# Scores of a 64 wide attention as two passes of 128 rows instead of three of 64

## The chip, the core and the metric

The kernel runs on one core of one Trainium2 chip. It is written by hand for the five engines of a core: TensorE (PE, matmuls), VectorE (DVE), ScalarE (ACT), GpSimd (POOL) and SyncE (SP, which here only begins transfers). Each engine works through its own queue of instructions in order, and the queues meet at semaphores. The metric is the time of one execution on the device, in microseconds (us); lower is better.

## The reference

It is a decoder of four layers on x of 8 x 256 x 256 in float32; each layer adds a gated cross attention to a context of 8 x 256 x 192 and a gated feed forward part of its own kind. The change lies in the third layer's cross attention, with 16 heads of 64:

```python
def _L2_xattn_ref(x, context, w_q, w_k, w_v, w_o, b_o):
    HEADS = 16
    DIM_HEAD = 64
    ...
    SCALE = DIM_HEAD ** (-0.5)
    q = (x @ w_q).reshape(B, Sq, HEADS, DIM_HEAD).transpose(0, 2, 1, 3)
    k = (context @ w_k).reshape(B, Skv, HEADS, DIM_HEAD).transpose(0, 2, 1, 3)
    v = (context @ w_v).reshape(B, Skv, HEADS, DIM_HEAD).transpose(0, 2, 1, 3)
    sim = jnp.einsum('bhid,bhjd->bhij', q, k) * SCALE
    attn = jax.nn.softmax(sim, axis=-1)
    out = jnp.einsum('bhij,bhjd->bhid', attn, v)
    out = out.transpose(0, 2, 1, 3).reshape(B, Sq, INNER)
    return out @ w_o + b_o
...
    x = x + jnp.tanh(g_xattn[2]) * _L2_xattn_ref(_layernorm(x, axis=-1), ctx_768, ...)
```

## The kernel before

The stages run one after the other: l0x, l0f, l1x, l1f, l2x, l2f, l3x, sim, l3f (an x is an attention, an f a feed forward part). The change edits l2x, which the class `Wide` plans and the functions `wide` of each engine carry out, and one load of weights for l3f.

Matmuls whose result must be close to float32 are done with operands split into two parts, a high part (rounded to the format fp32r) and a low part (the rest). `mm3` adds three passes: low by high, high by low, high by high. The product of the two low parts is left out.

l2x goes through 128 heads: 8 batch items of 16. Four neighbouring heads (index `u`) share one set of tiles: `keys2[u % 3]` and `queries2[u % 3]`, 128 partitions high, where an even head of each couple has partitions 0 to 63 and an odd one 64 to 127 (`e = i % 2`), and `k = i // 2 % 2` says which couple. For step i, TensorE's queue has in this order:

- `scores(i)`: for both halves of the queries (t) one `mm3` of 64 rows, 128 x 256 each, into bank i % 2; six matmuls
- `turn_probs(i - 3)`: four transposes (line 2005) of the normalised probabilities of head i - 3
- the jobs of step i: keys of u = i // 4 + 2 at i % 4 = 0, values (v) at 1, queries at 2, nothing at 3; in each item moreover at i % 16 = 5 and 6 the two halves of the output projection of the item before (`projected`, line 1979), and at 7 the transposes of the next item's rows
- at odd i, the product of probabilities and values for two heads (line 2020), which writes 64 columns at a time

VectorE in step i: the row maxima of head i (line 1037), the copy of the transposed probabilities of head i - 3 (line 1044), then what the jobs of step i - 1 ask for: `low_keys` (line 1052) or `low_queries` (line 1060); at i % 16 = 1 also `combine` (line 943, adding the mixture of the layer before) and the statistics for the next item; at 7 `finish`, whose first operation (line 1075, the sum with the bias) sets the bank of the output projection free. ScalarE: the high parts of keys and queries (`high_keys`, `high_queries`), copies of values and outputs, and the exponentials of head i (line 1620). GpSimd: division by the sum (lines 837 and 840), the splitting of the context, and at i % 16 = 3 four gathers of rows (line 769). SyncE begins the loads of the context, one for each item.

The products of jobs go to the banks 5, 6 and 7 in turn (`place`), and TensorE waits (`mf`) until the product that had the bank before has been read. The keys and queries of u are jobs eight and six steps ahead of the first scores that read them; `scores(i)` waits until the exponentials of head i - 2 have read its bank.

## Time and profile before

| | before |
|---|---|
| median of 3 runs | 2401.87 us (2387.91 to 2403.25) |
| the profiled execution | 2405.62 us |
| its span in the profile | 2403.9 us |
| mean granted TensorE clock | 0.868 of full speed |
| busy in the span: PE / PEld / DVE / ACT / POOL | 1970.7 / 1529.6 / 1316.6 / 769.3 / 782.9 us |
| HBM read and written | 89.26 and 47.19 MB |
| the l2x stage in the span | from about 1045 to 1513 us |

PE is the matmuls, PEld the loading of their stationary operand, which overlaps them. The profile is of one execution; its rows give starts and durations of instructions from the start of the span. The shares of busy time are over all stages together, and say little of one of them.

### The profile page before, as it was taken

How to read it: one execution, taken by the hardware profiler on the slowest of the kernel's cores; microseconds unless marked ns; L12 is line 12 of the kernel's file. 1: busy time of each engine (PE TensorE's matmuls, PEld its weight loads, DVE VectorE, ACT ScalarE, POOL GpSimd, SP SyncE). 2: the span in 40 equal slices, each digit the busy share in tenths (PEclk: the TensorE clock that was granted, in tenths of full speed). 3: DMA queues.
4: the chain of work that ended last, by engine and by line, in shares of the span. 5: the costliest groups of instructions: out<-in, count | busy, mean ns of one | idle time of the engine just before them, and what ended most of it. 6: DMA issues, size and time to landing. Idle time of an engine off the chain costs nothing.

```text
span 2403.9 us, 33562 instructions
## 1 busy us (share of the span) xinstructions
PE 1970.7 (82%) x12232; PEld 1529.6 (64%) x12232; DVE 1316.6 (55%) x2824; ACT 769.3 (32%) x1697; POOL 782.9 (33%) x694
## 2 busy tenths in 40 slices
PE   3589699942999999869999999599967888448997
PEld 2467566532777777757778787478855555336664
DVE  2434478551555444345555555565546898446773
ACT  1122146400222121134444444122322445112554
POOL 4110101054355444256666555454533200100000
PEclk9789679655999999879999999599985889776898
DMA  4280456123333332220000001034626542023341
GB/s 142 84 279 0 58 77 88 22 81 116 110 110 119 110 110 92 82 68 16 13 13 13 4 1 66 3 105 136 205 78 112 86 66 29 0 36 56 57 74 41
DMA packets 120190, 177.88 MB, mean 74 GB/s; under 512 B 10916, under 2 KB 105188, under 8 KB 117412
## 3 DMA queue, kind: packets, MB, share of 16 engines
q1 hardware_dynamic: 91092, 128.36, 23.4%
q0 software_dynamic: 8448, 26.52, 3.7%
q10 hardware_dynamic: 20496, 20.97, 2.6%
q8 instruction: 95, 1.56, 0.3%
q14 instruction: 59, 0.48, 0.1%
HBM read 89.26 MB, written 47.19 MB: 57 GB/s over the span
## 4 chain that ended last, share of the span: by engine, by line
PE 59%; issue 12%; DVE 11%; POOL 9%; DMA 5%; ACT 2%; SPq 1%; DVEq 0%; POOLq 0%; ACTq 0%
PE bank L1846 13%; PE bank L1847 10%; PE bank L1848 10%; PE bank L2125 5%; PE bank L2157 4%; POOL ewl L785 3%; DMA ew<-in_we 3%; PE bank L2005 3%; PE bank L2020 3%; PE bank L1979 2%; DVE nmf L1144 2%; PE bank L2142 1%; POOL ewh L783 1%; POOL rows_by_expert L797 1%; PE bank L2167 1%
## 5 line engine op out<-in xcount | busy, mean ns | idle before, releaser
L1144 DVE TENSOR_REDUCE nmf<-bank 128x2 f32<-128x512 f32 x384 | 260.8, 689 | 120.4 <-PE bank L2125 117.6
L1719 ACT ACTIVATE pT<-bank 128x512 f32<-128x512 f32 x384 | 224.8, 597 | 249.6 <-PE bank L2142 247.6
L1407 DVE TENSOR_TENSOR bank<-sil,bank 128x512 f32<-128x512 f32 x136 | 94.8, 697 | 285.0 <-ACT sil L1774 284.5
L2125 PE MATMUL bank<-kpack,qpack 48*128 48x256 f32 (+1 forms) x768 | 202.1, 370 | 53.6 <-DVE nmf L1144 30.9
L1846 PE MATMUL bank<-split,ewl 128*128 128x512 f32 x514 | 212.1, 413 | 24.2 <-POOL ewl L785 13.9
L1847 PE MATMUL bank<-split,ewh 128*128 128x512 f32 (+1 forms) x578 | 228.7, 396 | 0.0
L1848 PE MATMUL bank<-split,ewh 128*128 128x512 f32 (+1 forms) x578 | 227.7, 394 | 0.0
L2125 PEld LDWEIGHTS bank<-kpack,qpack 48*128 48x128 f32 (+1 forms) x768 | 128.6, 222 | 134.8 <-DVE nmf L1144 63.9
L785 POOL TENSOR_TENSOR ewl<-ew,ewh 128x1536 fp32r<-128x1536 f32 (+1 forms) x47 | 205.9, 4380 | 3.8
L2142 PE MATMUL bank<-qpack,kpack 50*128 50x256 f32 (+1 forms) x768 | 198.5, 359 | 9.2 <-ACT pT L1719 9.1
L783 POOL CAST ewh<-ew 128x1536 fp32r<-128x1536 f32 (+1 forms) x47 | 85.2, 1813 | 325.0 <-DMA ew<-in_we 314.3
L1037 DVE TENSOR_REDUCE nmax<-bank 128x2 f32<-128x512 f32 x128 | 88.5, 691 | 186.8 <-PE bank L1848 186.3
L1620 ACT ACTIVATE w<-bank,nmax 128x256 f32<-128x256 f32 x256 | 119.2, 471 | 223.1 <-DVE nmax L1037 223.0
L1774 ACT ACTIVATE sil<-bank 128x512 f32<-128x512 f32 x136 | 81.4, 598 | 322.0 <-PE bank L1848 322.0
L1846 PE MATMUL bank<-ewh,split 128*128 128x256 f32 x544 | 168.1, 309 | 6.6 <-issue 6.6
L1847 PE MATMUL bank<-ewl,split 128*128 128x256 f32 x544 | 156.6, 288 | 0.0
L1848 PE MATMUL bank<-ewh,split 128*128 128x256 f32 x544 | 156.1, 287 | 0.0
L724 POOL TENSOR_TENSOR rstd<-rstd,mhalf 128x2 f32<-128x2 f32 x40 | 28.5, 712 | 385.2 <-DVE rstd L1128 256.4
L837 POOL TENSOR_TENSOR esum<-esum,minus 128x2 f32<-128x2 f32 x128 | 89.3, 698 | 168.1 <-ACT w L1620 167.9
L840 POOL TENSOR_TENSOR w<-w,esum 128x512 f32<-128x512 f32 x128 | 137.0, 1070 | 10.1
L2142 PEld LDWEIGHTS bank<-qpack,kpack 50*128 50x128 f32 (+1 forms) x768 | 124.0, 212 | 24.5 <-ACT pT L1719 19.9
L1846 PEld LDWEIGHTS bank<-split,ewl 128*128 128x128 f32 x514 | 98.1, 191 | 63.2 <-DVE split L1410 21.1
(431 smaller groups left out, 4757.7 us busy)
## 6 DMA issues: line engine op xcount, KB each, us to landing
ew<-in_we SPq DMA_DIRECT2D x32, 768.0 KB, 7.8
ew<-in_we SPq DMA_DIRECT2D x15, 1408.0 KB, 6.2
rows_by_expert<-zeros ACTq DMA_DIRECT2D x1, 20480.0 KB, 62.5
kpack<-khl SPq DMA_DIRECT2D x144, 128.0 KB, 4.0
qpack<-qhl SPq DMA_DIRECT2D x144, 128.0 KB
arena<-rows_by_expert SPq DMA_DIRECT2D x23, 512.0 KB, 4.2
rows_by_expert<-arena SPq DMA_DIRECT2D x38, 256.0 KB, 5.5
ct<-in_ctxT SPq DMA_DIRECT2D x32, 192.0 KB, 2.4
```

The lines of the kernel that those rows point to most:

```text
L783: nc.gpsimd.tensor_copy(high, whole).then_inc(m["wh"], 1)
L785: nc.gpsimd.tensor_tensor(low, whole, high, ALU.subtract).then_inc(m["ws"], 1)
L840: nc.gpsimd.tensor_tensor(p3, p3, total.rearrange("p (t o) -> p t o", o=1).broadcast_to([P, T, S]), ALU.mult).then_inc(m["pn"], 1)
L1144: V.tensor_reduce(nmf[:, c, :, j, r], bank[s.banks[i % len(s.banks)]][:, :] .rearrange("p (t k) -> p t k", t=T), AXX, ALU.max, negate=True ...
L1620: ins = A(probs[i % 4][:, t * S:(t + 1) * S], bank[i % 2][:, t * S:(t + 1) * S], ACT.Exp, bias=nmax[:, h, t:t + 1], accum_out=esum[:, h, t ...
L1719: A(pT16[i % 8][:, :], bank[2 + h % 2][:, :], ACT.Exp, scale=s.qscale).then_inc(m["e"], 1)
L1846: mm(out_, al, bh, start=start, stop=False)
L1847: mm(out_, ah, bl, start=False, stop=False)
L1848: return mm(out_, ah, bh, start=False, stop=stop)
L2125: ins = mm(bank[s.banks[i % len(s.banks)]][:, t * S:(t + 1) * S], q[rows, r, t * P:(t + 1) * P], k[rows, r, :], start=True, stop=True)
L2142: ins = mm(bank[2 + h % 2][:, t * S:(t + 1) * S], k[rows, r, t * P:(t + 1) * P], q[rows, r, :], start=True, stop=True)
L2157: ins = mm(bank[4][j * 32:j * 32 + s.vs, gr % 2 * S:(gr % 2 + 1) * S], v16[n % 3][:, kt, h * s.vs:(h + 1) * s.vs], pT16[(n * NH + (h ^ 1)) ...
```

## The change

The high and the low part of the queries now stand above each other: for the even head of a couple the high part in partitions 0 to 63 and the low part in 64 to 127, for the odd head the other way round (`queries2[u % 3][e]`). The keys' high part stands in both halves, and their low part in the half of the queries' high part, with zeros in the other. Then two passes of 128 rows do what three of 64 did: (high and low queries) by (high keys twice), and (high and low queries) by (low keys and zeros).

The parts are written where they are made, in two instructions of 64 partitions each instead of one of 128, by ScalarE (high) and VectorE (low; the low queries to the other half than they are read from). The second copy of the keys' high part is made by transfers from SBUF to SBUF, two for each u, which SyncE begins when ScalarE has written the high keys (`kh`), and for which the first scores of u wait (`kd0` to `kd2`). The zeros are written once at the start of the stage by six copies on VectorE (`kz`). SyncE's loads of the context move into the same loop. The tiles take more room: `rows3`, which now lies over `raw3`, holds some of the queries, and so the three loads of the l3f weights into `raw3` move from the kernel's start (line 718) to GpSimd's part of the l2f stage.

```diff
@@ -264,7 +265,8 @@
         raw1 = w13[:, 0:6 * D].rearrange("p (w c f) -> p w c f", w=3, c=DC)
-        raw3 = sb("raw3", [P, 3, DC, D])
+        raw3 = under("raw3", [P, 3, DC, D])
+        rows3 = sb("rows3", [P, 3 * DC * D], F32R)
         onx = [w13[0:NX, b * D:(b + 1) * D] for b in range(4)]
@@ -390,8 +392,10 @@
         wv2 = split[0:CK, 8192:8192 + 4 * inner].rearrange("p (w c f) -> p w c f", w=2, c=2)
-        keys2 = [t.rearrange("p (w g s) -> p w g s", w=2, g=2) for t in threes(0, 4 * S)]
-        queries2 = [t.rearrange("p (w g s) -> p w g s", w=2, g=2) for t in threes(3072, 4 * S)]
+        keys2 = [t.rearrange("p (e w g s) -> p e w g s", e=2, w=2, g=2) for t in threes(0, 8 * S)]
+        queries2 = [[t[:, o + e * 512:o + e * 512 + 512].rearrange("p (g s) -> p g s", g=2) for e in range(2)]
+                    for t, o in ((split, 6144), (rows3, 0))]
+        queries2.append([t[:, o:o + 512].rearrange("p (g s) -> p g s", g=2) for t, o in ((split, 7168), (rows3, 1024))])
         values2 = [arena[:, 12288 + k * 1024:13312 + k * 1024].rearrange("p (t n) -> p t n", t=T) for k in range(3)]
@@ -436,14 +440,14 @@
 
-        names = ("x_in", "w0_in", "w0f_in", "att_in", "consts", "tanh", "phase", "out_done", "w3_in", "w2a_in", "w2b_in", "w2c_in",
+        names = ("x_in", "w0_in", "w0f_in", "att_in", "consts", "tanh", "phase", "out_done", "w3_in", "w2a_in", "w2b_in", "w2c_in", "w4_in",
                  "xn", "xnT", "xt", "rq", "rd", "zero", "masked")
...
 
-        wx = group("l2x", "ct", "cs", "wh", "wl", "xh", "kh", "qh", "s", "mx", "e", "psum", "pn", "pT", "pTc", "pv", "oc", "dve",
+        wx = group("l2x", "ct", "cs", "wh", "wl", "xh", "kh", "kd0", "kd1", "kd2", "kz", "qh", "s", "mx", "e", "psum", "pn", "pT", "pTc", "pv", "oc", "dve",
                    "mp0", "mp1", "mp2", "mf0", "mf1", "mf2")
@@ -631,10 +635,16 @@
             if "l2x" in run:
-                for n in range(B):
-                    if n > 0:
-                        sp.wait_ge(wx["cs"], 2 * n)
-                    sp.dma_start(ct[:, :, :], a["ctxT"][n, :, :, :]).then_inc(wx["ct"], 16)
+                sp.dma_start(ct[:, :, :], a["ctxT"][0, :, :, :]).then_inc(wx["ct"], 16)
+                for u in range(L2X.pairs):
+                    sp.wait_ge(wx["kh"], u + 1)
+                    for e in range(2):
+                        own, other = slice(64 * e, 64 * e + 64), slice(64 - 64 * e, 128 - 64 * e)
+                        sp.dma_start(keys2[u % 3][other, e, 0, :, :].bitcast(F32),
+                                       keys2[u % 3][own, e, 0, :, :].bitcast(F32)).then_inc(wx[f"kd{u % 3}"], 16)
+                    if u % 4 == 0 and u // 4 + 1 < B:
+                        sp.wait_ge(wx["cs"], 2 * (u // 4 + 1))
+                        sp.dma_start(ct[:, :, :], a["ctxT"][u // 4 + 1, :, :, :]).then_inc(wx["ct"], 16)
             if "l2f" in run:
@@ -708,7 +718,7 @@
             later2 = [(raw2[0], a["wq_l2x"]), (raw2[1], a["wk_l2x"]), (raw2[2], a["wv_l2x"]), (wo["l2x"], a["wo_l2x"])]
-            loads += [(raw3[:, 0, :, :], a["wq_l3f"]), (raw3[:, 1, :, :], a["wk_l3f"]), (raw3[:, 2, :, :], a["wv_l3f"])]
+            later3 = [(raw3[:, 0, :, :], a["wq_l3f"]), (raw3[:, 1, :, :], a["wk_l3f"]), (raw3[:, 2, :, :], a["wv_l3f"])]
             loads += [(bo[n][:, :], a[f"bo_{n}"].partition_broadcast(P)) for n in ("l2x", "l3x", "l3f")]
@@ -802,6 +812,8 @@
                         pool.dma_start(dst, src).then_inc(g["w3_in"], 16)
+                    for dst, src in later3:
+                        pool.dma_start(dst, src).then_inc(g["w4_in"], 16)
                 for w in range(s.ring, s.sets):
@@ -874,6 +886,7 @@
                     root(sm, 2, ss[:, 0:NH], ss[:, 0:NH], mhalf[:, 0:NH])
+                    pool.wait_ge(g["w4_in"], 16 * 3)
                     split_packed(L3F)
@@ -1049,7 +1062,10 @@
                     src = from_[:, :].rearrange("p (g s) -> p g s", g=2)
-                    tt(keys2[u % 3][:, 1, :, :], src, keys2[u % 3][:, 0, :, :], ALU.subtract).then_inc(done, 1)
+                    for e in range(2):
+                        own = slice(64 * e, 64 * e + 64)
+                        ins = tt(keys2[u % 3][own, e, 1, :, :], src[own, :, :], keys2[u % 3][own, e, 0, :, :], ALU.subtract)
+                    ins.then_inc(done, 1)
 
@@ -1057,8 +1073,10 @@
                     src = from_[:, :].rearrange("p (g s) -> p g s", g=2)
-                    stt(queries2[u % 3][:, 1, :, :], src, s.qscale, queries2[u % 3][:, 0, :, :], ALU.mult, ALU.subtract)\
-                        .then_inc(done, 1)
+                    for e in range(2):
+                        own, other, to = slice(64 * e, 64 * e + 64), slice(64 - 64 * e, 128 - 64 * e), queries2[u % 3][e]
+                        ins = stt(to[other, :, :], src[own, :, :], s.qscale, to[own, :, :], ALU.mult, ALU.subtract)
+                    ins.then_inc(done, 1)
 
@@ -1081,6 +1099,11 @@
                 normal(0)
+                for u in range(3):
+                    for e in range(2):
+                        other = slice(64 - 64 * e, 128 - 64 * e)
+                        V.tensor_copy(keys2[u][other, e, 1, :, :], zeros[other, :, :].broadcast_to([64, 2, S]))\
+                            .then_inc(m["kz"], 1)
                 for i in range(s.FIRST, s.last):
@@ -1591,13 +1614,19 @@
                         act.wait_ge(m["s"], 4 * (u - 2))
-                    copy(keys2[u % 3][:, 0, :, :], groups(from_)).then_inc(m["kh"], 1)
+                    for e in range(2):
+                        own = slice(64 * e, 64 * e + 64)
+                        ins = copy(keys2[u % 3][own, e, 0, :, :], groups(from_)[own, :, :])
+                    ins.then_inc(m["kh"], 1)
 
...
                         act.wait_ge(m["s"], 4 * (u - 2))
-                    A(queries2[u % 3][:, 0, :, :], groups(from_), ACT.Copy, scale=s.qscale).then_inc(m["qh"], 1)
+                    for e in range(2):
+                        own = slice(64 * e, 64 * e + 64)
+                        ins = A(queries2[u % 3][e][own, :, :], groups(from_)[own, :, :], ACT.Copy, scale=s.qscale)
+                    ins.then_inc(m["qh"], 1)
 
@@ -1983,16 +2012,18 @@
                     u, k, e = i // 4, i // 2 % 2, i % 2
+                    if i == 0:
+                        pe.wait_ge(m["kz"], 6)
                     if i % 4 == 0:
...
                         filled(("q", u))
+                        pe.wait_ge(m[f"kd{u % 3}"], 32 * (u // 3 + 1))
                     if i >= 2:
                         pe.wait_ge(m["e"], i - 1)
-                    r = slice(64 * e, 64 * e + 64)
-                    for t in range(T):
-                        ins = mm3(bank[i % 2][:, t * S:(t + 1) * S],
-                                  [queries2[u % 3][r, w, k, t * P:(t + 1) * P] for w in range(2)],
-                                  [keys2[u % 3][r, w, k, :] for w in range(2)], True, True)
+                    for t in range(T):
+                        for w in range(2):
+                            ins = mm(bank[i % 2][:, t * S:(t + 1) * S], queries2[u % 3][e][:, k, t * P:(t + 1) * P],
+                                     keys2[u % 3][:, e, w, k, :], start=w == 0, stop=w == 1)
                     ins.then_inc(m["s"], 1)
```

TensorE's queue at the first scores of the second set (head 3, then head 4 of the first item; `split` and `rows` hold keys and queries, `ewh,ewl` are the query projections ahead, `ident,w` the transposes of probabilities). Before:

```order
L1848 MATMUL bank<-ewh,ewl 128x256
L1846 MATMUL bank<-split 128x256 [waits l2x_e]
L1847 MATMUL bank<-split 128x256
L1848 MATMUL bank<-split 128x256
...
L2005 MATMUL bank<-ident,w 128x128 [waits l2x_pn]
L2005 MATMUL bank<-ident,w 128x128 x3
L1846 MATMUL bank<-split 128x256 [waits l2x_e,l2x_mf0,l2x_mf1]
```

And in the changed kernel:

```order
L1877 MATMUL bank<-ewh,ewl 128x256
L2025 MATMUL bank<-split 128x256 [waits l2x_e]
L2025 MATMUL bank<-split 128x256 x3
L2036 MATMUL bank<-ident,w 128x128 [waits l2x_pn]
L2036 MATMUL bank<-ident,w 128x128 x3
L2025 MATMUL bank<-split,rows 128x256 [waits l2x_kd1,l2x_e,l2x_mf0,l2x_mf1]
```

Four matmuls stand in the place of six, and the first of a set has the transfers (`kd1`) among its waits.

VectorE's queue at the start of the stage, from behind the first normalised rows (`xn`) on (`ewh` are the low parts of the turned rows, `split` and `rows` the low keys and queries, `x<-w` the sums of `combine`). Before:

```order
L1032 TENSOR_SCALAR xn<-x,mv,rstd 128x256
L1068 TENSOR_TENSOR ewh<-bank,ewh 128x512 [waits l2x_xh,l2x_mp0]
L1052 TENSOR_TENSOR split<-bank,split 128x512 [waits l2x_kh,l2x_mp1]
L1060 SCALAR_TENSOR_TENSOR split<-bank,split 128x512 [waits l2x_qh,l2x_mp0]
...
L1037 TENSOR_REDUCE nmax<-bank 128x2 [waits l2x_s] x2
L1052 TENSOR_TENSOR split<-bank,split 128x512 [waits l2x_kh,l2x_mp1]
L943 SCALAR_TENSOR_TENSOR x<-w,gw_l1f,x 128x256 [waits mo_gt1]
```

And in the changed kernel:

```order
L1045 TENSOR_SCALAR xn<-x,mv,rstd 128x256
L1105 CAST split<-zeros 64x512 x6
L1086 TENSOR_TENSOR ewh<-bank,ewh 128x512 [waits l2x_xh,l2x_mp0]
L1067 TENSOR_TENSOR split<-bank,split 64x512 [waits l2x_kh,l2x_mp1]
L1067 TENSOR_TENSOR split<-bank,split 64x512
L1078 SCALAR_TENSOR_TENSOR split<-bank,split 64x512 [waits l2x_qh,l2x_mp0]
L1078 SCALAR_TENSOR_TENSOR split<-bank,split 64x512
...
L1050 TENSOR_REDUCE nmax<-bank 128x2 [waits l2x_s] x2
L1067 TENSOR_TENSOR split<-bank,split 64x512 [waits l2x_kh,l2x_mp1]
L1067 TENSOR_TENSOR split<-bank,split 64x512
```

Six copies of zeros have come in ahead of the low rows, and each low key or query operation has become two of half the height, of which the second pair shown now stands ahead of `combine`.

## Rows read from the trace of the kernel before

**Rows 1.** Stretch: us, busy PE, PEld, DVE, ACT, POOL, clock, DMA share, GB/s.

```profile
1172.00:1228.00 56.00, 56.00 (x380) 44.80 (x378) 31.97 (x58) 25.30 (x81) 34.29 (x40) 1.00 0.05 14
```

**Rows 2.** The chain that ended last: start us, us, what; l2x, output projection.

```profile
1185.85 3.46 PE bank L1979 x16
...
1242.11 3.46 PE bank L1979 x16
```

**Rows 3.** Timeline of PE, an odd head's scores: start, us, engine, line.

```profile
1209.08 0.28 PE L1848 MATMUL bank<-ewh,ewl 128*128 128x256 f32 x1
1209.29 0.38 PE L1846 MATMUL bank<-split 64*128 64x256 f32 x1
1209.52 0.28 PE L1847 MATMUL bank<-split 64*128 64x256 f32 x1
...
1209.99 0.27 PE L1848 MATMUL bank<-split 64*128 64x256 f32 x1
1210.19 0.66 PE L2005 MATMUL bank<-ident,w 128*128 128x128 f32 x4
```

**Rows 4.** Timeline of PE, start of l2x: queries end, keys of 96 rows begin.

```profile
1055.48 0.28 PE L1848 MATMUL bank<-ewh,ewl 128*128 128x256 f32 x1
1055.60 0.28 PE L1846 MATMUL bank<-ewh,ewl 96*128 96x256 f32 x1
1055.72 0.28 PE L1847 MATMUL bank<-ewh,ewl 96*128 96x256 f32 x1
```

**Rows 5.** Timeline of PE: four transposes that follow other transposes.

```profile
1198.02 0.60 PE L1970 MATMUL bank<-ident,xn 128*128 128x128 f32 x4
```

**Rows 6.** One VectorE line, two heights: ns min/median/max, first and last start.

```profile
L1407 DVE TENSOR_TENSOR bank<-sil,bank x136: 695/697/706, 594.3 to 1777.2; 128x512 f32<-128x512 f32 x121, 64x512 f32<-64x512 f32 x15
```

**Rows 7.** Timeline: head 1's scores begin, head 2's exponentials end, head 4's scores.

```profile
1170.69 0.38 PE L1846 MATMUL bank<-split 64*128 64x256 f32 x1
...
1178.73 0.20 ACT L1620 ACTIVATION_READ_ACCUMULATOR w<-bank,nmax 128x1 f32 x1
...
1179.99 0.38 PE L1846 MATMUL bank<-split 64*128 64x256 f32 x1
```

**Rows 8.** Timeline: head 7's maxima, bias sum of the output, key matmuls at head 8.

```profile
1197.63 0.69 DVE L1037 TENSOR_REDUCE nmax<-bank 128x2 f32<-128x512 f32 x1 [5.09 <-PE bank L1848]
...
1199.43 0.68 DVE L1075 TENSOR_TENSOR scr<-bank,bo_l2x 128x512 f32<-128x512 f32 x1
...
1200.88 0.36 PE L1846 MATMUL bank<-ewh,ewl 96*128 96x256 f32 x1
```

**Rows 9.** Transfers: KB each and median us to landing; six issues on SP's queue.

```profile
kpack<-khl SPq DMA_DIRECT2D x144, 128.0 KB, 4.0
...
276.52 3.92 SPq L594 DMA_DIRECT2D kpack<-khl  x6
```

**Rows 10.** Timeline of the stage's start: normalised rows, high keys, first queries, first scores.

```profile
1048.48 0.73 DVE L1032 TENSOR_SCALAR xn<-x,mv,rstd 128x256 f32<-128x256 f32 x2 [2.70 <-POOL rstd L724]
...
1052.97 0.60 ACT L1545 ACTIVATE split<-bank 128x512 fp32r<-128x512 f32 x1 [1.90 <-PE bank L1848]
...
1054.16 0.28 PE L1846 MATMUL bank<-ewh,ewl 128*128 128x256 f32 x1
...
1059.96 0.38 PE L1846 MATMUL bank<-split 64*128 64x256 f32 x1
```

**Rows 11.** Timeline of PE at head 6; the stretch around it.

```profile
1079.03 0.66 PE L2005 MATMUL bank<-ident,w 128*128 128x128 f32 x4 [1.57 <-POOL w L840]
...
1077.00:1091.00 14.00, 12.43 (x71) 10.06 (x71) 5.26 (x9) 5.24 (x16) 11.48 (x15) 0.76 0.09 25
```

**Rows 12.** Timeline of PE in the last eight heads: the longest wait there.

```profile
1484.61 0.65 PE L2020 MATMUL bank<-arena 128*64 128x256 f32 x4 [1.14 <-ACT w L1545]
```

**Rows 13.** The chain of waits at the kernel's start.

```profile
17.97 1.61 POOL raw L718 x3
...
26.44 2.95 POOL rstda L724
```

## The prediction

> **What bounds the kernel now.** I read the table of stretches first. In a stretch of 56 us in the middle of the l2x stage (the only stage whose loops the change edits) TensorE's matmuls are busy for all of it at the full granted clock, 2.4 GHz, while VectorE has work for 32 us, GpSimd for 34, ScalarE for 25 and the DMA engines for 5% [rows 1]. The chain of waits says the same: inside this stage it holds TensorE lines alone, and its row for the 16 output-projection matmuls comes back after 1242.11 - 1185.85 = 56.26 us [rows 2]. That is one batch item, 16 heads, so a head costs 3.52 us. What a head's matmuls cost is therefore what the stage costs, until another wait takes over.
>
> Next the timeline of one head [rows 3]. Inside a run of 256-column matmuls with 128 or 96 rows the starts lie 0.12 us apart, also where a run with other operands begins [rows 4]. The score batch has 64 rows and is different at both its ends. The first score matmul starts 1209.29 - 1209.08 = 0.21 us after the last query matmul, and the second 0.23 after the first: with 0.12 as the normal step this is 0.09 + 0.10 too much (other batches show 0.22 for the second). At the other end the transposes start 0.20 after the last score matmul, 0.08 too much, and four of them take 0.66 us, where four that follow transposes take 0.60 [rows 5]: 0.06 more. So a 64-row batch costs about 0.19 us on entry and 0.14 on exit, beside its six matmuls. An even head is entered from the value matmuls, which write only 64 columns, so that its entry is a change of shape either way. The Trainium skill (TensorEngine Tiling (Array Packing), Tiling Modes, Key Properties) says that changing the tiling mode drains the engine; the trace agrees, with the sizes above.
>
> **The change on TensorE.** (a) Two passes fewer for each half of the queries: 6 matmuls become 4, so a head saves 2 x 0.118 = 0.236 us. The new ones have 128 rows, whose step is 0.12 instead of 0.118; for 64 in a batch item I take off 0.1 us. (b) With 128 rows the exit from the scores to the transposes is no change of shape: 0.14 us a head. (c) The entry is none either at odd heads, where key or query matmuls come before: 0.19. At even heads the 64-column value matmuls still come before, and I leave the entry as it is. An even head saves 0.376 us, an odd one 0.566; 16 heads save 8 x 0.942 - 0.1 = 7.4 us. Without (b) and (c) it would be 3.7.
>
> **What it adds, and who waits.** Key and query parts are now written in two instructions of 64 partitions. An operation of VectorE on 64 partitions takes as long elsewhere as on 128, 695 to 706 ns over both forms [rows 6], and I take the same for ScalarE; so each of the two engines issues one more operation of 0.6 to 0.7 us for keys and one for queries, four times four heads: some 5 us of VectorE and 5 of ScalarE in 50, well inside their idle time. In order, though, two places come late:
>
> Head 2 of each item. After head 1's maximum VectorE does the low keys, then the sums of the previous layer and the statistics, and only then head 2's maximum. From head 1's first score matmul, 1170.69, to the end of head 2's exponentials, 1178.93, is 8.24 us; head 4's scores, which write the same bank, start at 1179.99, 9.30 after [rows 7]. The shorter batch takes 0.34 from the first number (0.10 + 0.236), the second key operation adds 0.6: 8.50, and 0.12 for the semaphore makes 8.62. TensorE would arrive at 9.30 - 0.476 - 0.376 - 0.566 = 7.88. New stall: 0.74 us.
>
> Head 8. The key matmuls after its transposes take the PSUM bank that VectorE frees with the bias sum of the output (L1075). From head 7's maximum, 1197.63, that sum ends at 1200.11, 2.48 after, and the key matmuls start at 1200.88, 3.25 after [rows 8]. With a second low-query operation ahead (0.6) and 0.1 for the semaphore the bank is free at 3.18; TensorE arrives at 3.25 - 0.14 - 0.376 = 2.73. New stall: 0.45 us.
>
> So an item costs 56.26 - 7.4 + 1.2 = 50.0 us, a gain of 6.2.
>
> The copies of the keys' high part: SyncE has nothing else queued then but the next context, whose wait is over by that time. Two issues at 3.92/6 = 0.65 us each and 4.0 us from issue to landing for 128 KB of the same kind (SBUF to SBUF) [rows 9] give some 5.5 us after ScalarE is done. The scores that read them come seven heads after, 7 x 3.05 = 21 us: hidden, at no cost. At head 0, where nothing has been built up, ScalarE begins the high keys at 1052.97 and is done with two operations by 1054.2, the second copy lands 0.65 + 4.0 later, near 1058.9, and the first scores begin at 1059.96 [rows 10]: 1 us to spare. The Trainium skill (DMA: Bandwidth & Descriptors, Anatomy of one DMA) has about 2 us of fixed cost for a DMA, which would only widen that margin; the row is of copies that queue behind each other, and is the one used.
>
> The six copies of zeros stand on VectorE between the first normalised rows and the first low rows. The trace has no such copy. Bounded by nothing and by 0.7 us each (a vector operation of this width, [rows 6]), they end 0 to 4.2 us after 1049.2, the low rows 0.7 later, by 1054.1 at the latest, and the queries that read those start at 1054.16 [rows 10]: between 0 and 0.1 us. I take 0.
>
> **Edges of the stage.** Heads 0 to 6 of the first item gain nothing: the transposes at 1079.03 wait 1.57 us for GpSimd [rows 11], which has four gathers ahead of that product, and that queue is paced by VectorE's sums. Heads 7 to 15: 0.476 + 4 x 0.376 + 4 x 0.566 = 4.2. Six items from head 16 to head 111: 6 x 6.2 = 37.3. Heads 112 to 119, which have no sums to wait for: 3.8. In the last eight heads there are no key or query matmuls left as cover, and every fourth head already waits for the output copy behind its exponentials [rows 12]; there a pair gains 0.33 instead of 0.94, so 2 x 0.33 + 2 x 0.94 = 2.5, and 2.4 with the odd start. Sum 47.7 us.
>
> **Outside the stage.** Three loads of l3f weights leave the start of GpSimd's queue, 1.61 us, and directly behind that queue stands the root that the first stage waits for, on the chain [rows 13]: 1.6 us gained. They come back in the l2f stage, behind the last scatter, where GpSimd next waits for weights that are loaded only once an expert is done: 0.
>
> Sum: 47.7 + 1.6 = 49.3. From the profiled execution's 2405.62 that gives 2356.3; its time is 3.75 above the median of the three, 2401.87, from which I forecast **2353 us**.
>
> **Rivals.** A, only the matmul count matters: the gaps at the ends of the batch belong to the semaphore waits there, not to the 64 rows. Then an item saves 3.7, with nearly no new stall (head 4: 9.30 - 3 x 0.236 = 8.6 against 8.6), so 6 x 3.6 + 9 x 0.236 + 8 x 0.236 + 1.5 + 1.6 = 28.7: 2373. Against it stand the key matmuls of [rows 4], which also begin behind waits and have no gap. 12%.
>
> B, the new stalls lower TensorE's clock. After the 1.57 us of idling the mean granted clock of 14 us was 0.76 [rows 11]: part of them passed at 1.2 GHz instead of 2.4, which lost 14 x 0.24 = 3.4 us of work. One such fall in each of six items gives back 20 us: 2373; two give 2393. Against it: a wait of 1.14 us in the last heads [rows 12] did not do it, and mine are 0.74 and 0.45. 8%. The Trainium skill (TensorE: Matmul & The Clock Gate, Part 1) tells of such falls after idle gaps; no gap of 0.7 us shows one here.
>
> C, slower: the copies land late. TensorE would wait at every fourth head for the landing. What is asked for seven heads ahead paces four heads at 4/7 of the landing time, and this exceeds today's 14.07 us for four heads from 24.6 us of landing on; at 26 us the stage would be some 25 us longer and the time 2427. The row says 4.0, and the engines are 5% busy. 2%.
>
> D, better: even heads lose their entry gap as well, 0.19 x 60 = 11 us: 2342. 7%.
>
> **How the numbers follow.** The forecast with its own errors (the new stalls between 0 and 2.5 us an item instead of 1.2, some 7 us either way, and about 2 for the edges) spans 2343 to 2363 and has 68%; another 3% are causes I can't name. The range of 8 in 10 leaves out C and the far end of B: 2341 to 2374. A measurement tells some 1% from no change, 24 us. Faster by more: the forecast, D and nearly all of A and B, 93%; within 1%: 5%; slower: 2%.
>
> **What would show it.** In the profile after: item period near 50.0 us in the chain; 512 score matmuls 0.12 apart, with no gap to the transposes; a gap of 0.1 left at even heads; waits of TensorE of 0.7 us for the exponentials at head 4 and 0.45 at head 8 in six items; no wait for the copies, with landings near 4 us; the root on GpSimd 1.6 us earlier. The forecast fails if the gaps stay (A), if the clock row falls below 1.00 in mid-stage (B), or if VectorE's half-height operations that move between halves take clearly more than 0.7 us.

## The result and the profile after

The changed kernel takes 2365.43 us, the median of four runs (2360.91 to 2370.63); the kernel before takes 2396.46 on the same chip (2387.91 to 2403.25). The ratio is 0.9873, with a 95% interval of 0.9842 to 0.9903: 31 us less. The forecast was 2353, a gain of 49 from a median of 2401.87 for the kernel before; a fourth run has since brought that median down by 5.4, so the time missed by 12 us and the gain by 18. The time is inside the range, but the gain is two thirds of what was forecast, and in the l2x stage, where it was to arise, it is smaller by a third too.

The profiled execution took 2362.5 us (span 2360.8, mean clock 0.869; before 2405.62, 2403.9 and 0.868). Stage by stage, from the marks of the two traces: the first root on GpSimd starts at 24.73 instead of 26.44; from the first statistics of l2x to the root of l2f it is 1473.69 - 1036.4 = 437.3 us instead of 1514.82 - 1045.5 = 469.3. That makes 1.7 + 32.0 = 33.7. The rest of the 43.1 us between the two spans comes from stages whose code is the same (3.4, 4.0, 0.8, -9.4 and 10.6 us): they scatter from one execution to the next, and nothing below rests on them.

First a head without disturbance, an odd one, on the timeline of PE. It answers to [rows 3]:

```profile
1142.63 0.28 PE L1877 MATMUL bank<-ewh,ewl 96*128 96x256 f32 x1
1142.75 0.64 PE L2025 MATMUL bank<-split,rows 128*128 128x256 f32 x4
1143.22 0.60 PE L2036 MATMUL bank<-ident,w 128*128 128x128 f32 x4
```

The score batch begins 0.12 us after the last key matmul, lasts 0.47 us (four steps of 0.12) and is followed by transposes that take 0.60. The gaps of 0.09 and 0.10 at its start and of 0.08 and 0.06 at its end are gone. An even head keeps the gap at its start, behind the value matmuls: there the batch shows 0.74 instead of 0.64.

The stage as a whole doesn't look like that. One batch item in a stretch of the table of windows, which answers to [rows 1], and below it the chain of waits, which answers to [rows 2] (its pieces of under 0.2 us are left out, as are longer ones at the marks):

```profile
1099.00:1150.70 51.70, 48.98 (x351) 40.87 (x349) 38.47 (x66) 29.60 (x90) 34.14 (x39) 1.00 0.14 35
```

```profile
1102.59 0.47 ACT split L1568
1103.07 0.30 ACT split L1568
1103.36 0.38 issue
1103.75 0.68 DVE split L1067
1104.44 0.69 DVE split L1067
1105.17 1.71 DVE x L956 x2
1106.91 0.88 DVE x L956 x2
...
1109.10 0.70 DVE nmax L1050
...
1110.44 1.08 PE bank L2051 x8
...
1116.36 3.46 PE bank L2008 x16
...
1168.03 3.46 PE bank L2008 x16
```

The period is 1168.03 - 1116.36 = 51.67 us (forecast 50.0, before 56.26), and TensorE is busy for 48.98 us of 51.7. Before, the chain held TensorE alone. Now at head 2 of every item it goes through ScalarE's two high-key copies, VectorE's two low-key operations, the sums of the previous layer (L956) and the statistics, and comes back to TensorE at a value product. (Its last link, of 0.2 us, lies on head 2's exponentials; but the value product waits in the code for `pTc`, VectorE's copy of turned probabilities, and the rows below name it.) The timeline of PE gives the size of that wait, and the view of PE's waits for 1036 to 1470 us (line that waited, on what; us in total, times, longest) how often it comes:

```profile
1110.44 1.08 PE L2051 MATMUL bank<-sil,arena 128*64 128x256 f32 x8 [2.11 <-DVE sil L1057]
```

```profile
PE bank L2051 <- DVE sil L1057: 13.4, 7, 2.1
PE bank L2025 <- ACT w L1649: 5.8, 2, 5.0
PE bank L2051 <- ACT w L1568: 4.3, 2, 3.2
PE bank L1875 <- DVE scr L1093: 3.7, 6, 0.6
```

Six of the seven in the first row are 2.11 us long, one in each item. The last row is the wait at head 8 that was forecast at 0.45. The second is mostly in the first item, where head 4 waits 5.0 us for the exponentials of head 2 (0.65 before), and the third in the last eight heads.

### The profile page after: what moved, and what is told of

Its sections match the earlier page's. It is cut to its first block, busy times and chain, and to the rows that moved or that the text cites. A ratio compares the mean times of both kernels' runs of the same rounds, so it can differ in the third digit from the quotient of the medians.

```text
span 2360.8 us, 33280 instructions
## 1 busy us (share of the span) xinstructions
PE 1904.9 (81%) x11976; PEld 1489.9 (63%) x11976; DVE 1368.9 (58%) x2894; ACT 803.2 (34%) x1761; POOL 779.7 (33%) x694
## 3 DMA queue, kind: packets, MB, share of 16 engines
q8 instruction: 93, 1.52, 0.3%
## 4 chain that ended last, share of the span: by engine, by line
PE 54%; issue 14%; DVE 13%; POOL 10%; DMA 5%; ACT 3%; SPq 1%; DVEq 0%; POOLq 0%; ACTq 0%
PE bank L1875 10%; PE bank L1876 8%; PE bank L1877 8%; PE bank L2156 6%; PE bank L2188 4%; POOL ewl L795 3%; DMA ew<-in_we 3%; PE bank L2008 2%; DVE nmf L1167 2%; PE bank L2025 2%; PE bank L2051 2%; PE bank L2173 1%; PE bank L2036 1%; POOL ewh L793 1%; POOL rows_by_expert L807 1%
```

## Experiments

Most readings below use the item period, from VectorE's bias sum of one item to that of the next (L1093, before L1075). It repeats within 0.04 us wherever the clock stays up, so it tells tenths of a microsecond where the medians tell 5 or 10. In the kernel before all six periods are 56.26; in the changed one they are 51.67, 53.21, 51.66, 51.68, 51.67 and 49.48. The last belongs to an item with no sums of a next one behind head 1: it is 2.19 us shorter, so the kernel itself holds the first hint.

**1. The sums one step later.**

```diff
-                    if i % 16 == 1 and 1 <= (i + 15) // 16 < B:
-                        combine(L1F, (i + 15) // 16, ch)
-                        statistics((i + 15) // 16)
+                    if i % 16 == 2 and 1 <= i // 16 + 1 < B:
+                        combine(L1F, i // 16 + 1, ch)
+                        statistics(i // 16 + 1)
```

> The changed kernel, with VectorE's combine and statistics of the next item one loop step later (behind the maximum and the turned copy of the loop step in which the value product of head 3's step finds its input). Baseline: the changed kernel at 2365.4 us, item period 51.67, step from head 3 to head 4 4.20 us. Theory 1 (the missing gain sits in VectorE's queue: half-height writers plus combine hold back the turned copy for which the value product waits 2.11 us): that wait goes, the step from 3 to 4 falls to 2.0 to 2.1; maximum 3 is late instead, and the scores of head 5 wait 0.5 to 1.3 us for its exponent. Item period 50.2 to 51.1, time 2353 to 2361. Rival 1 (it sits in ScalarE's halved writers, or PE pays for something that the trace hides): moving combine only moves the wait, item period stays at 51.5 to 51.9, time within 3 us of 2365. Rival 2 (the shorter stall is not on the path, other waits fill it): step 3 to 4 falls but the item period does not.

2359.44 us (2355.97 to 2360.58), ratio 0.9858 (0.9812 to 0.9903). The step from head 3 to head 4 fell from 4.20 to 2.02 us, and no value product waits for VectorE any more. But maximum 3 came late instead, then exponentials 3 to 5; the step from head 5 to head 6 grew from 6.86 to 7.90, with a new wait of the output projection for ScalarE's output copy, six times:

```profile
PE bank L2008 <- ACT w L1568: 4.5, 6, 0.7
PE bank L1875 <- DVE scr L1093: 3.7, 6, 0.6
PE bank L2051 <- ACT w L1568: 3.2, 1, 3.2
```

Item 50.54: of the 2.19 us, 1.13 were won back. The wait belongs to where the sums stand in VectorE's queue; the victim of the new place was another than I had named (the scores of head 5).

**2 and 3. Passes and rows apart.** Three passes of 128 rows, from the changed kernel (the low part of the keys counts twice in the scores):

```diff
-                        for w in range(2):
+                        for j, w in enumerate((0, 1, 1)):
                             ins = mm(bank[i % 2][:, t * S:(t + 1) * S], queries2[u % 3][e][:, k, t * P:(t + 1) * P],
-                                     keys2[u % 3][:, e, w, k, :], start=w == 0, stop=w == 1)
+                                     keys2[u % 3][:, e, w, k, :], start=j == 0, stop=j == 2)
```

> The changed kernel with a third matmul of 128 rows per tile (the low part of the keys counted twice in the scores), so three passes as before, but no 64-row matmul in the scores. Theory 1 (the gaps of 0.14 and 0.19 us belong to the 64-row layout): plain steps stand at 2.45+0.24=2.69, 2.02+0.24=2.26 and 3.40+0.24=3.64 where the kernel before has 2.93, 2.50 and 3.87; the stall of 2.11 us in each item shrinks to about 1.4 since PE is 0.7 us later by then. Item 51.67+3.8-0.7=54.8 against 56.26 before; time 2365+8*3.1=2390, 3 to 9 us under before. Rival 1 (the gaps belong to the waits at the heads' edges and not to the rows): plain steps as before, 2.93 and 2.50, the time at or above before. Rival 2 (stalls are independent of PE's pace): 2365+30=2396.

Two passes of 64 rows, from the kernel before (the product of low queries and high keys is left out):

```diff
-                        ins = mm3(bank[i % 2][:, t * S:(t + 1) * S],
-                                  [queries2[u % 3][r, w, k, t * P:(t + 1) * P] for w in range(2)],
-                                  [keys2[u % 3][r, w, k, :] for w in range(2)], True, True)
+                        for w in range(2):
+                            ins = mm(bank[i % 2][:, t * S:(t + 1) * S], queries2[u % 3][r, 0, k, t * P:(t + 1) * P],
+                                     keys2[u % 3][r, w, k, :], start=w == 0, stop=w == 1)
```

> The kernel before with the pass of low queries by high keys left out: two passes of 64 rows, nothing else changed (scores lack that product). Theory 1 (a pass is worth 0.236 us a head, the gaps stay): plain steps 2.93-0.24=2.69, 2.50-0.24=2.26, 3.87-0.24=3.63; the chain on VectorE is the old one (copy ready 0.5 us before its use, now 0.7 us earlier wanted), so a stall of 0.2 to 0.4 us a period. Item 56.26-3.8+0.3=52.8; time 2396-8*3.5=2368, 24 to 31 us under before. Rival 1 (gaps belong to waits): the same time, but then the run with three passes of 128 rows gains nothing. Rival 2 (the passes are the whole gain of the changed kernel): its steps are 2.45 and 2.02 and the item 51.7.

Timeline of PE at the same odd head, with three passes of 128 rows:

```profile
1148.37 0.28 PE L1877 MATMUL bank<-ewh,ewl 96*128 96x256 f32 x1
1148.49 0.88 PE L2025 MATMUL bank<-split,rows 128*128 128x256 f32 x6
1149.21 0.60 PE L2036 MATMUL bank<-ident,w 128*128 128x128 f32 x4
```

and with two of 64:

```profile
1141.87 0.28 PE L1848 MATMUL bank<-ewh,ewl 96*128 96x256 f32 x1
1142.08 0.73 PE L1994 MATMUL bank<-split 64*128 64x256 f32 x4
1142.74 0.66 PE L2005 MATMUL bank<-ident,w 128*128 128x128 f32 x4
1143.15 0.48 PE L1846 MATMUL bank<-split,ewh 96*128 96x512 f32 x1
```

Six matmuls of 128 rows have no gap at either end; four of 64 rows still have 0.21 us on entry and the longer exit. The waits at the heads' edges are the same in both, so the gaps belong to the rows. That settles rival A.

| | item, us | median, us | ratio (95%) |
|---|---|---|---|
| three passes of 64 rows (before) | 56.26 | 2396.9 | 1 |
| two passes of 64 rows | 52.50 | 2375.54 | 0.9931 (0.9904 to 0.9959) |
| three passes of 128 rows | 54.42 | 2387.64 | 0.9968 (0.9941 to 0.9995) |
| two passes of 128 rows (changed) | 51.67 | 2365.4 | 0.9873 (0.9842 to 0.9903) |

The pass alone gives 3.76 us an item, 16 x 0.236 = 3.78 as costed, and no wait of TensorE above 0.45 us appears with it in the items: the old VectorE queue is just fast enough for that pace. The rows alone give 1.84, with the value product waiting 1.2 us at head 3. Together they give 4.59 and not 5.6, because the faster TensorE runs into the longer queue. By the medians the pass alone gains 21 us (a little under the 24 to 31 expected) and the rows alone 9.

**4. No copies.** SyncE's two transfers for each four heads and the wait for them are out; the other half of the keys' high part holds zeros, written by six more copies at the stage's start, so one product is left out of the scores.

```diff
-                        sp.dma_start(keys2[u % 3][other, e, 0, :, :].bitcast(F32),
-                                       keys2[u % 3][own, e, 0, :, :].bitcast(F32)).then_inc(wx[f"kd{u % 3}"], 16)
...
-                        pe.wait_ge(m[f"kd{u % 3}"], 32 * (u // 3 + 1))
```

> The changed kernel without the 64 transfers of the keys' high part and without the wait for them (the other half holds zeros, so the product of low queries by high keys is left out; VectorE has three more zeroing pairs in the stage's beginning). Theory 1 (the transfers land 2.5 us after their issue, more than 10 us before their use, and cost nothing): within 3 us of the changed kernel, 2362 to 2369, item period 51.67 to 0.1. Rival (the transfers load the SBUF or the queue and slow the engines' accesses, or delay the context load): item 0.3 to 1 us shorter, time 2357 to 2363.

2366.28 us (2362.07 to 2376.19), undisturbed item 51.68. The copies cost nothing, as forecast. The page of the changed kernel gives their landing (KB each, median us):

```profile
split<-split SPq DMA_DIRECT2D x64, 128.0 KB, 2.5
```

**5. The sums three steps later**, behind head 4's maximum and copy and ahead of TensorE's two long steps; GpSimd's root two loop steps later, the normalised rows one.

```diff
-                    if i % 16 == 1 and 1 <= (i + 15) // 16 < B:
+                    if i % 16 == 4 and 1 <= i // 16 + 1 < B:
...
-                    if i % 16 == 5 and 1 <= (i + 11) // 16 < B:
+                    if i % 16 == 6 and 1 <= i // 16 + 1 < B:
...
-                    if i % 16 == 3 and 1 <= (i + 13) // 16 < B:
+                    if i % 16 == 5 and 1 <= i // 16 + 1 < B:
```

> The changed kernel with VectorE's combine and statistics of the next item three loop steps later (behind the copy of the fourth head's step, in front of PE's two long steps), the item's root on GpSimd two later, its normalised rows one later. Theory 1 (the stall is VectorE's queue at that place alone, and one loop step was too little because the exponents then hold back the gathered copy that the output projection waits for): step 3 to 4 2.0, step 5 to 6 back from 7.90 to 6.9, item 51.67-2.18=49.5 (0 to 0.3 more where a new wait of that size shows at the item's rows); time 2365-7*2.1=2350, 2346 to 2354. Rival (combine costs the same wherever it stands, since VectorE is short of time in the whole first half of an item): item 50.5 or more, time at or above that of the run with combine one step later, 2358 or more.

2349.51 us (2346.71 to 2353.07), ratio 0.9805 (0.9758 to 0.9853). All six periods are 49.48, the 2.19 us are back to the hundredth. The step from head 3 to 4 is 2.02, that from 5 to 6 is 6.85, and maximum 5, now 3.25 us behind its scores instead of 0.75, makes nobody wait. In the first item head 4 waits 1.1 us instead of 5.0. The same instructions on the same engine: their place decided. Not all of that need be the queue's order, though. In the old place two of the four sums take 1.71 us and two 0.88 (the chain above); one of them, begun at 1105.57, takes 1.30 us where the others take 0.48, and ends 0.28 us behind this product on GpSimd:

```profile
1105.55 1.04 POOL L852 TENSOR_TENSOR w<-w,esum 128x512 f32<-128x512 f32 x1
```

It is so in each of the six items, and in the kernel before (1.19 us, begun later in the product, again 0.28 behind its end) too. In the new place all four take 0.48, so the block is 0.95 us shorter, 2.98 instead of 3.93. No run keeps the sums where they were without that overlap, so how the 2.19 us divide between order and overlap isn't shown.

**6. The bias sum first.** VectorE frees the bank before the low queries and adds to x one step later (`added` is the gated add, split off from `finish`). The gated add of the last item is left out here and in the next run.

```diff
+                    if i % 16 == 7 and 0 <= i // 16 - 1:
+                        finish(i // 16 - 1)
                     for what, n in s.jobs(i - 1):
...
-                    if i % 16 == 7 and 0 <= i // 16 - 1:
-                        finish(i // 16 - 1)
                     if i % 16 == 8 and 0 <= i // 16 - 1:
+                        added(i // 16 - 1)
                         stats_of(i // 16 - 1)
```

> The changed kernel with VectorE's bias sum of the item's result ahead of the low queries, and its gated add one loop step later, ahead of the next stage's statistics. Theory 1 (key matmuls at head 8 wait 0.62 us for the bank that this sum frees): that wait goes, step 8 to 9 falls from 3.31 to 2.7, item 51.1; in the last heads the maximum of head 120 stands 0.75 us earlier, the value product's wait of 3.19 falls to 2.4, with or without the fall of TensorE's clock behind it. Time 2365-6*0.6-1 to 3 = 2360, 2357 to 2363. Rival (that wait is filled by another one, the x transposes or the exponents): item 51.6, time within 2 of 2365.

2351.94 us (2349.55 to 2354.01), ratio 0.9818 (0.9771 to 0.9865); item 50.80 to 50.83, 0.87 less than in the changed kernel, and the step from head 8 to 9 is 2.45 instead of 3.31. The wait at head 8 was on the path and nothing filled it. The median fell by more than the expected 5 us; the item gives 6 x 0.87 = 5.2, and the rest I can't place, since it is within what untouched stages scatter.

**7. Both orders.**

> Both orders together. Theory 1: the gains add up: item 49.5-0.6=48.9, time 2365-15-5=2345, 2340 to 2350, under the changed kernel by 15 us or more. Rival (the gains overlap, since the wait at head 8 is fed by combine's delay): 2350 or more.

2345.52 us (2340.04 to 2350.32), ratio 0.9786 (0.9749 to 0.9823); item 48.62, so the gains add up: 51.67 - 2.19 - 0.87 = 48.61. Between heads 16 and 111 TensorE has no wait above 0.45 us left.

**8. The start alone**, from the kernel before: the three loads moved, with the wait for them, and nothing else.

> The kernel before with the three loads for the last attention stage issued where the changed kernel issues them, and the wait for them in the similarity stage; nothing else. Theory 1 (the loads delayed the first rows of the start): the start's root begins at 24.7 to 24.9 us instead of 26.44, the rest is as before, 2394 to 2405 (a single run can't tell 1.6 us, the mark can). Rival (the 1.7 us of the changed kernel's start come from chance): it begins at 26.0 to 26.6.

```profile
24.08 0.54 POOL L718 DMA_DIRECT2D qg<-in_qg  x1
24.63 2.95 POOL L724 TENSOR_TENSOR rstda<-rstda,mhalf 128x16 f32<-128x16 f32 x1
```

The root starts at 24.63 instead of 26.44 [rows 13]: 1.8 us from the three loads. (One run of 2396.92 us.) Its l2x stage has the same code as the kernel before and serves below as a second execution of it.

**9. The cut writers alone**, from the kernel before: each of the four writers as two instructions of 64 rows, here one of them:

```diff
-                    tt(keys2[u % 3][:, 1, :, :], src, keys2[u % 3][:, 0, :, :], ALU.subtract).then_inc(done, 1)
+                    for e in range(2):
+                        own = slice(64 * e, 64 * e + 64)
+                        ins = tt(keys2[u % 3][own, 1, :, :], src[own, :, :], keys2[u % 3][own, 0, :, :], ALU.subtract)
+                    ins.then_inc(done, 1)
```

> The kernel before with each of the four writers of the keys' and queries' parts (two on ScalarE, two on VectorE) cut into two instructions of 64 rows, targets and scores as before. It prices what the changed layout costs these two engines alone. Theory 1 (a half-height instruction costs as much as a whole one, 0.69 on VectorE and 0.59 on ScalarE, and in front of combine this sits in the path to the value product, whose input was ready 0.5 us early): VectorE's copy comes 0.69 later by its own and 0.4 by the wait for ScalarE, so the value product waits 0.5 to 0.7 us an item; item 56.8 to 57.0 against 56.26, time 4 to 6 over before. Rival (half the rows cost about half): item 56.26, no change.

2443.73 us (2433.77 to 2446.33) beside 2418.45 for the kernel before on that chip, ratio 1.0100 (1.0066 to 1.0135). Item 57.04, 0.78 more, as expected; the whole is 25 us slower where 4 to 6 were expected. The stage itself takes 483.1 us against 469.3 in the first trace of before: 4.2 of the 13.8 come from six items, 4.5 from the last eight heads and 5.0 from the first item. In the latter two a wait grew and TensorE's clock fell behind it (in the first item 3.9 us of waiting and some 10 at half clock, where the kernel before waits 1.57 and falls for less [rows 11]). Table of windows (the third column from the end is the granted clock):

```profile
1065.00:1070.00 5.00, 1.11 (x7) 1.06 (x6) 3.81 (x11) 2.17 (x7) 1.03 (x2) 0.93 0.00 0
1070.00:1080.00 10.00, 10.00 (x42) 7.92 (x40) 6.73 (x10) 4.76 (x15) 8.74 (x11) 0.52 0.18 53
...
1489.20:1499.40 10.20, 10.04 (x40) 6.76 (x41) 3.68 (x6) 3.07 (x13) 6.54 (x8) 0.50 0.02 9
```

At the end the wait for the output copy is 2.1 us where it was 1.14 [rows 12], and some 10 us at half clock follow, where the kernel before had none there. Where the remaining 11 us are, the trace doesn't say: there is no profile of the kernel before on this chip, on which the untouched l2f stage up to its last weight casts takes 293 us instead of 269. Outside the l2x stage no trace shows a price of the cut writers: that rest takes 1923.5 us in the changed kernel and 1934.6 in the kernel before, and on this chip 1958.9 in run 9 and 1961.1 and 1963.2 in runs 10 and 11.

**10 and 11. Both orders complete, and ScalarE's output copy ahead of the exponent.** The first has the last item's gated add behind the loop. The second adds:

```diff
-                    if 0 <= i < s.heads:
-                        exponent(i)
                     if i % 4 == 0 and 0 <= i // 4 - 2 < s.pairs:
                         gathered(i // 4 - 2)
+                    if 0 <= i < s.heads:
+                        exponent(i)
```

> The two orders together (combine three loop steps later, bias sum first and gated add one step later) with the gated add of the last item, which the earlier run of both orders left out, put behind the loop. Theory 1: item 48.62 as there, the add costs up to 0.75 us at the end of the stage and may bring the next stage's statistics later by as much: 2343 to 2349. Rival (the left out add hid more than its own time): above 2350.

> The same, with ScalarE's output copy ahead of the exponent in each fourth loop step instead of behind it. Theory 1 (in the last eight heads a value product waits 3.19 us for this copy, which stands behind an exponent whose maximum is late, and TensorE's clock falls behind that wait): the wait goes or falls under 1 us, no fall of the clock behind it, the stretch from the bias sum of head 119's step to the next stage's root falls from about 34 to 30 to 32; the items stay at 48.62 since the copy fits before the exponent there; 2 to 4 us under the kernel without it, 2340 to 2345. Rival (the wait is only handed to the exponents, which then come 0.6 us later): the stretch stays at 34, the time is the same or some 0.6 us an item longer.

On the slower chip of run 9: 2373.72 (ratio 0.9811, 0.9780 to 0.9842) and 2371.80 (0.9802, 0.9770 to 0.9835). Both have items of 48.62. From the bias sum of head 119's step to the next root it is 34.94 us in the first and 33.62 in the second: 1.3 us saved, less than the 2 to 4 expected. The wait of 2.4 us for the copy is gone and the clock stays up, but waits of 1.0 to 1.4 us for GpSimd, VectorE and the exponentials take its place. The medians can't tell the two apart. Windows of the tail, first of run 10, then of run 11:

```profile
1424.00:1428.00 4.00, 3.02 (x16) 2.27 (x17) 3.04 (x6) 1.85 (x7) 2.58 (x4) 0.70 0.57 238
```

```profile
1424.00:1428.00 4.00, 3.67 (x29) 2.90 (x29) 3.07 (x6) 2.84 (x12) 3.49 (x5) 1.00 0.02 8
```

Run 11 has the lowest ratio with all of the computation: against the kernel before, each on its chip, it stands at 0.980 where the changed kernel stands at 0.987. Runs 5 (only the sums moved) and 10 are as good within the error.

## Why the prediction was right in kind and too high in size

**Right.** The bound, and the price of an undisturbed head: 0.236 for the passes (3.76 an item against 3.78), the gaps at both ends of a 64-row batch, the even head's entry left as it is. With both stalls moved away (runs 7, 10 and 11) an item costs 48.62 us, so passes and rows are worth 56.26 - 48.62 = 7.64; the term was 7.4. Heads 112 to 119 gained 3.83 (forecast 3.8), the start 1.7 (1.6). The copies never made anyone wait. Their landing was 2.5 us where I took 4.0 from copies that queue; the Trainium skill (DMA: Bandwidth & Descriptors, Anatomy of one DMA) gives about 2 us of fixed cost, for transfers that GpSimd issues, and is close to what these from SyncE show.

**Near by luck: the first sixteen heads**, 3.45 measured (from the statistics on) for 4.2. The start of the stage lost 0.5 us, where I took the zero copies as free. Heads 0 to 6, which were to gain nothing, lost 2.4 with the wait of 5.0 us at head 4. Heads 7 to 15 gained 6.4, because TensorE's clock fell just there in the trace of before, and in the changed kernel it fell earlier and partly while TensorE waited. Windows of before, of the same code in run 8, where it didn't fall, and of the changed kernel:

```profile
1080.00:1086.80 6.80, 6.80 (x32) 5.30 (x30) 2.40 (x4) 2.22 (x6) 6.56 (x8) 0.50 0.12 31
```

```profile
1070.20:1084.00 13.80, 13.72 (x99) 11.18 (x100) 7.31 (x12) 6.26 (x20) 12.03 (x15) 1.00 0.05 15
```

```profile
1064.50:1068.30 3.80, 3.80 (x18) 3.80 (x19) 2.67 (x4) 2.55 (x9) 3.28 (x4) 0.50 0.02 4
```

From the statistics to head 16's scores it is 66.0 us in the trace of before, 63.7 in run 8 and 62.5 in the changed kernel: against run 8 the gain is 1.2 and not 3.45.

**The step that failed: "Head 2 of each item", New stall 0.74 us; measured 2.11 (2.19 an item).** Two errors: the waiter (1.3 us for 0.74) and the length of the queue (2.11 for 1.3).

First, the wrong waiter. I followed VectorE's late maximum 2 to its exponentials and from there to head 4's scores. Directly behind that maximum VectorE copies the turned probabilities, and the value product of head 3's step takes them. In the kernel before it had 0.5 us of slack, the copy ending at 1177.79 + 0.68 = 1178.47, against 1.1 for the path that I costed [rows 7]:

```profile
1177.79 0.68 DVE L1044 COPY sil<-bank 128x512 f32<-128x512 f32 x1
```

```profile
1178.97 0.87 PE L2020 MATMUL bank<-sil,arena 128*64 128x256 f32 x6
```

From head 1's first score matmul the copy ended 7.78 us later, and the product began 8.28 later. With my own terms that makes 7.78 - 0.34 + 0.6 + 0.12 = 8.16 for the copy, and 8.28 - 0.476 - 0.376 - 0.566 = 6.86 for TensorE: a stall of 1.3 us from the numbers I had. In the changed kernel the exponentials that I followed end at 1110.84, 0.6 us before head 4's scores, which come right behind the value product:

```profile
1110.64 0.20 ACT L1649 ACTIVATION_READ_ACCUMULATOR w<-bank,nmax 128x1 f32 x1
```

```profile
1111.45 0.75 PE L2025 MATMUL bank<-split 128*128 128x256 f32 x4
```

Second, the queue was longer than costed. From maximum 1 to maximum 2 it grew from 5.50 to 7.02 us, by 1.52, where I had 0.6 (0.72 with the semaphore behind it). Timeline of VectorE:

```profile
1102.08 0.69 DVE L1050 TENSOR_REDUCE nmax<-bank 128x2 f32<-128x512 f32 x1 [0.43 <-PE bank L2025]
1102.68 0.68 DVE L1057 COPY sil<-bank 128x512 f32<-128x512 f32 x1
1103.75 1.39 DVE L1067 TENSOR_TENSOR split<-bank,split 64x512 fp32r<-64x512 f32 x2 [0.38 <-issue]
1105.17 2.62 DVE L956 SCALAR_TENSOR_TENSOR x<-w,gw_l1f,x 128x256 f32<-128x256 f32 x4
```

The low keys start 1.67 us after the maximum, before 1.21, since ScalarE's second high-key copy isn't done (0.46); they hold VectorE for 1.42 us, before 0.59 (0.83, where I had 0.6); the sums and statistics take 3.93 instead of 3.70 (0.23). I had counted ScalarE's extra operation as hidden in its idle time. It isn't, because VectorE's next instruction waits for it.

**Head 8**: 0.45 forecast, 0.62 measured as a wait and 0.87 as what its removal gives (runs 6 and 7). With 2.19 that makes 3.06 of stalls for 1.2, and 7.64 - 3.06 = 4.58, the measured 4.59. For six items 37.3 became 6 x 4.59 = 27.5.

**Rival B came true in small.** Behind one of the six waits of 2.11 us TensorE's clock fell, which cost that item 1.55 us:

```profile
1211.00:1213.70 2.70, 0.66 (x6) 0.42 (x5) 2.56 (x10) 0.54 (x3) 0.00 (x0) 1.00 0.00 0
...
1214.70:1218.60 3.90, 3.90 (x21) 3.81 (x20) 2.88 (x5) 2.68 (x10) 3.35 (x5) 0.56 0.00 0
```

So six items gave 27.5 - 1.5 = 26.0 instead of 37.3. My condition for B, that the new stalls be longer than the known harmless 1.14 us, fits this; I gave it 8% because I had sized them at 0.74.

**The last eight heads**: +2.4 forecast, 1.2 us lost (by the scores of head 120 to the root). The wait for the output copy, 1.14 before, is 3.19 now and the clock falls behind it. The copy stands behind an exponent, this behind head 120's maximum, and this on VectorE behind two low-query operations, the bias sum and the gated add (0.75 us from 1440.18):

```profile
1438.03 1.39 DVE L1078 SCALAR_TENSOR_TENSOR rows<-bank,rows 64x512 fp32r<-64x512 f32 x2
...
1439.45 0.69 DVE L1093 TENSOR_TENSOR scr<-bank,bo_l2x 128x512 f32<-128x512 f32 x1
...
1440.96 0.69 DVE L1050 TENSOR_REDUCE nmax<-bank 128x2 f32<-128x512 f32 x1
...
1443.34 1.62 PE L2051 MATMUL bank<-arena 128*64 128x256 f32 x8 [3.19 <-ACT w L1568]
```

I had priced only the shorter batches there and had not seen that the longer writers stand in the tail too. Run 9 has the same wait growing to 2.1 with TensorE's work unchanged, so the writers alone are enough for it.

The sum: 3.45 + 26.0 + 3.8 - 1.2 = 32.0 in the stage for 47.7, and 1.7 at the start. Luck had a part in the range's holding. The forecast's own band, 2343 to 2363, allowed the stalls 2.5 us an item; they are 2.73 as waits and 3.06 by their removal, and the time lies just above that band. It is inside the wider range, which was drawn up to 2374 for rival A and the near end of B, neither of which is what happened at their size. The fourth run of the kernel before, which lowered the baseline by 5.4 us, brought the time nearer to the forecast than the gain was.

What stays open: the cost of the cut writers over the whole kernel (25 us by the medians of run 9, 13.8 by the stage's marks), and what the stall at head 2 would be without the overlap with GpSimd.

## What to carry to other kernels

When a change lengthens a queue, list everything that is issued behind the added instruction and follow each to its consumer; the one with the least slack decides, and it need not be the most prominent. An extra operation on an engine with idle time is free only if no other engine waits for its end. A block of work without a near deadline belongs ahead of the bound engine's longest step: moved there, the same instructions gave back 2.19 us an item. Look also at what the other engines do at the old place and the new: here the block itself became 0.95 us shorter.

## What the runs showed of the hardware

- An instruction of 64 partitions costs what one of 128 does: 0.69 us on VectorE, also where it writes to the other half of the partitions than it reads (two low-query operations 1.39), and 0.59 on ScalarE.
- A sum of `combine` on VectorE (128x256) takes 0.47 to 0.49 us in all traces, except where it starts well inside a product of 1.04 us (128x512) on GpSimd: then it ends 0.28 us behind that product, however early it began, and takes up to 1.30. That VectorE waits there for GpSimd is read from these times; no run tests it by itself.
- TensorE's clock falls at waits of 1.5 to 5 us in some cases and not in others that look the same. Of the 18 waits of 2.11 us in the changed kernel and runs 4 and 6, four were followed by a longer item (52.3 to 53.2 us instead of 50.8 or 51.7), and in each of the four the trace shows half the clock for 3.4 us. None of the waits of 1.2 us in run 2 was. After 3.19 us the clock fell in the changed kernel, and behind the same wait of 3.20 in run 4 it did not; after 1.57 us it fell in the trace of before [rows 11], and after 1.56 us in run 8, of the same code, not. The Trainium skill (TensorE: Matmul & The Clock Gate, Part 1) tells of falls after idle gaps; the traces agree, and show that the length of the gap alone doesn't decide.
- Untouched code differs between chips: the l2f stage up to the same mark takes some 269 us in ten traces and 293 to 294 in the three from the chip of runs 9 to 11, at whole times that differ by 1%. Compare ratios across chips, never times.
